# First half of the attention rows mixed through float16 halves, the low halves made by VectorE out of PSUM

## The reference

```python
x = x + 0.5 * ffn(layernorm(x))       # router: 16 experts, top 4
x = x + attention(layernorm(x))
x = x + 0.5 * ffn(layernorm(x))

def attention(x):                     # 8 batches, S = 1024, d = 128
    Q, K, V = x @ Qw, x @ Kw, x @ Vw
    scores = einsum('bqd,bkd->bqk', Q, K) / sqrt(d) + causal mask
    return einsum('bqk,bkd->bqd', softmax(scores), V)
```

## Time and profile before

| | |
|---|---|
| time, median of 3 runs | 674.87 us (673.19 to 675.13) |
| the profiled execution | 673.13 us |
| its span | 671.3 us, so 1.8 us lie around the span |
| PE busy | 634.8 us, 95% |
| DVE busy | 552.5 us, 82% |
| ACT busy | 554.3 us, 83% |
| POOL busy | 521.8 us, 78% |

### The profile page before, as it was taken

One profiled execution on the slowest core, in us unless ns is written; L12 is line 12 of the kernel. 1 busy time (PEld: TensorE's weight loads), 2 busy tenths in 40 slices (PEclk: granted clock), 3 DMA queues, 4 the chain that ended last, 5 costly groups with the idle time before them and its releaser, 6 DMA issues.

```text
span 671.3 us, 15215 instructions
## 1 busy us (share of the span) xinstructions
PE 634.8 (95%) x3395; PEld 493.3 (73%) x3395; DVE 552.5 (82%) x2562; ACT 554.3 (83%) x1187; POOL 521.8 (78%) x411
## 2 busy tenths in 40 slices
PE   4689999999999999699998999999999999999997
PEld 3557777777777776578787787777777777777775
DVE  4898999898998986568777688878999898899863
ACT  3479889898888899888888877679888888988975
POOL 3379989889999887756556656569999989998976
PEclk9999999999999999899999999999999999999999
DMA  9866677765678760344344443975678887677882
GB/s 240 200 149 129 143 153 160 162 145 129 143 151 172 154 139 1 68 94 85 72 94 78 86 90 59 209 146 129 146 171 169 178 172 165 145 168 166 178 173 73
DMA packets 107801, 92.05 MB, mean 137 GB/s; under 512 B 59488, under 2 KB 73456, under 8 KB 107760
## 3 DMA queue, kind: packets, MB, share of 16 engines
q1 hardware_dynamic: 105552, 91.00, 64.1%
q10 hardware_dynamic: 2208, 0.59, 0.4%
HBM read 72.70 MB, written 5.24 MB: 116 GB/s over the span
## 4 chain that ended last, share of the span: by engine, by line
PE 76%; DVE 10%; ACT 5%; issue 4%; POOL 3%; DMA 1%; POOLq 0%; DVEq 0%; ACTq 0%
PE psum L1373 20%; PE psum L1374 19%; PE psum L1375 19%; PE psum L1446 4%; PE psum L1404 2%; PE psum L1458 2%; DVE w_raw L1255 2%; PE psum L1626 2%; POOL shared L544 1%; PE psum L1420 1%; ACT zn L779 1%; PE psum L1585 1%; PE psum L1610 1%; PE psum L1594 1%; PE psum L1611 1%
## 5 line engine op out<-in xcount | busy, mean ns | idle before, releaser
L452 POOL TENSOR_TENSOR shared_r<-shared,shared_r 128x512 fp32r<-128x512 f32 x256 | 326.4, 1296 | 46.0 <-ACT shared L642 43.5
L1109 DVE SCALAR_TENSOR_TENSOR s_sb<-psum,wb 128x512 f32<-128x512 f32 x256 | 175.6, 688 | 44.7 <-PE psum L1375 25.2
L642 ACT ACTIVATE shared<-s_sb 128x512 f32<-128x512 f32 x288 | 177.8, 619 | 22.8 <-DVE s_sb L1109 22.8
L641 ACT ACTIVATE shared_r<-s_sb 128x512 fp32r<-128x512 f32 x256 | 159.8, 624 | 33.9 <-DVE s_sb L1109 31.9
L1373 PE MATMUL psum<-x_hi,w_hi 128*128 128x512 f32 x288 | 125.8, 437 | 1.5 <-issue 0.9
L1373 PE MATMUL psum<-shared_r,w_hi 128*128 128x512 f32 x256 | 114.6, 447 | 0.5 <-POOL shared_r L452 0.5
L1375 PE MATMUL psum<-x_hi,w_lo 128*128 128x512 f32 x288 | 113.8, 395 | 0.0
L1374 PE MATMUL psum<-x_lo,w_hi 128*128 128x512 f32 x288 | 113.5, 394 | 0.0
L1374 PE MATMUL psum<-shared_r,w_hi 128*128 128x512 f32 x256 | 101.4, 396 | 0.0
L1375 PE MATMUL psum<-shared_r,w_lo 128*128 128x512 f32 x256 | 100.7, 393 | 0.0
L544 POOL TENSOR_TENSOR shared<-s_sb,shared 128x1024 f16<-128x1024 f32 (+3 forms) x32 | 56.7, 1771 | 48.3 <-ACT shared L572 48.3
(11 more groups left out here) (169 smaller groups left out, 1372.4 us busy)
## 6 DMA issues: line engine op xcount, KB each, us to landing
wb<-scratch SPq DMA_DIRECT2D x128, 512.0 KB, 8.1
out<-x_sb SPq DMA_DIRECT2D x16, 256.0 KB, 9.8
x_sb<-in_L_attn_x SPq DMA_DIRECT2D x4, 256.0 KB, 6.4
scratch<-wT SPq DMA_DIRECT2D x32, 32.0 KB, 1.9
w_raw<-in_L_ffn_W ACTq DMA_DIRECT2D x1, 512.0 KB, 6.0
w_raw<-in_L_ffn_W SPq DMA_DIRECT2D x1, 512.0 KB, 6.9
wb<-shared SPq DMA_TRANSPOSE x32, 4.0
w_raw<-in_L_ffn_Ws ACTq DMA_DIRECT2D x1, 64.0 KB, 8.9
```

The costliest lines, as they stand in the source:

```text
L452: nc.gpsimd.tensor_tensor(g_lo[:, j % RING, :], g_f[:, j % RING, :], g_hi[:, j % RING, :].bitcast(F32), ALU.subtract).then_inc(F.glo_done, 1)
L641: nc.scalar.activation(g_hi[:, j % RING, :], s_sb[:, j % RING, :], ACT.Square)
L642: nc.scalar.activation(g_f[:, j % RING, :], s_sb[:, j % RING, :], ACT.Square).then_inc(F.sq_done, 1)
L1109: ins = nc.vector.scalar_tensor_tensor(s_, h_, 0.0, wb[:, u, c, :], ALU.max, ALU.mult)
```

## The change

Four things change, all in attention and all for the soon rows.

1. `pT` keeps the same bytes but holds float16 pairs. ACT's `pT_copy` now writes the high half (scaled by 2^15, undone when the mixed rows are copied out).
2. A new DVE operation for each soon tile, `pT_lo`, reads `tp_ps` and the high half and writes the low half. Tile by tile it reads 512, 384, 256 and 128 columns.
3. PE's `prob_transpose` and `mix` wait for DVE's low half (`pTlo_done`) where they waited for ACT's copy (`pT_done`).
4. `mix` makes three float16 matmuls with `zn16` for each key tile instead of one float32 matmul; for `zn16` POOL's `z16_halves` gets one more wait, and `mix` one.

```diff
-        pT = w_raw[:, 0:HQ * HQ * P].rearrange("p (k q) -> p k q", k=HQ)
+        pT = w_raw[:, 0:HQ * HQ * P].bitcast(F16).rearrange("p (k s q) -> p k s q", k=HQ, s=2)
...
                     wait(pool, A.pair_done[PAIRS[1]], b - 1)
+                    if half == 0:
+                        wait(pool, A.mix_done, b - 1)
...
-                    copy(pT[:, 0:t + 1, q0:q0 + P], tp_ps[:, 0:(t + 1) * P].rearrange("p (k q) -> p k q", q=P)).then_inc(A.pT_done, 1)
+                    copy(pT[:, 0:t + 1, 0, q0:q0 + P], tp_ps[:, 0:(t + 1) * P].rearrange("p (k q) -> p k q", q=P), scale=P_SCALE).then_inc(A.pT_done, 1)
...
+                def pT_lo(b, t):
+
+                    q0 = t * P
+                    v.wait_ge(A.pT_done, HQ * b + SOON.index(t) + 1)
+                    nc.vector.scalar_tensor_tensor(pT[:, 0:t + 1, 1, q0:q0 + P], tp_ps[:, 0:(t + 1) * P].rearrange("p (k q) -> p k q", q=P), P_SCALE,
+                                                   pT[:, 0:t + 1, 0, q0:q0 + P], ALU.mult, ALU.subtract).then_inc(A.pTlo_done, 1)
...
                         for s in range(QT):
+                            if b > 0 and s == 0:
+                                pT_lo(b - 1, SOON[2])
                             row_max(b, s)
+                            if b > 0 and s == 2:
+                                pT_lo(b - 1, SOON[3])
+                            if s == 6:
+                                pT_lo(b, SOON[1])
...
                             if b + 1 < B and s in (5, 7):
                                 q_lo_part(b + 1, (7 - s) // 2, prep_ps)
+                            if s == 5:
+                                pT_lo(b, SOON[0])
...
+                    pT_lo(B - 1, SOON[2])
                     start_ffn(16)
                     finish(B - 2, 0)
                     for c in range(AHEAD):
...
                         lead_ffn(c)
+                        if c == 0:
+                            pT_lo(B - 1, SOON[3])
...
                 def prob_transpose(b, t):
                     pe.wait_ge(A.exp_done, QT * b + PLACE[t] + 1)
-                    wait(pe, A.pT_done, HQ * b + SOON.index(t))
+                    wait(pe, A.pTlo_done, HQ * b + SOON.index(t))
...
                 def mix(b):
 
-                    pe.wait_ge(A.pT_done, HQ * (b + 1))
+                    pe.wait_ge(A.pTlo_done, HQ * (b + 1))
+                    pe.wait_ge(A.z16lo_done[0], b + 1)
...
-                        ins = mm(u_home(b, 0)[:, k * P:], zn(b, 0)[:, k, :], pT[:, k, k * P:], start=(k == 0), stop=(k == HQ - 1))
+                        out_, p_hi, p_lo = u_home(b, 0)[:, k * P:], pT[:, k, 0, k * P:], pT[:, k, 1, k * P:]
+                        mm(out_, zn16[b % 2][:, 0, k, :], p_hi, start=(k == 0), stop=False)
+                        mm(out_, zn16[b % 2][:, 0, k, :], p_lo, start=False, stop=False)
+                        ins = mm(out_, zn16[b % 2][:, 1, k, :], p_hi, start=False, stop=(k == HQ - 1))
```

More of the change, by code:

```diff
@@ L41 @@
 Z_SCALE = 2.0 ** 11
-PROB_SHIFT = 15 * math.log(2.0)
+P_SCALE = 2.0 ** 15
+PROB_SHIFT = math.log(P_SCALE)
 RSQRT_GUESS = 0x5f3759df
@@ L110, in __init__ @@
         self.pT_done = sem("a_pT_done")
+        self.pTlo_done = sem("a_pTlo_done")
         self.mix_done = sem("a_mix_done")
@@ L746, in uT_copy @@
                     wait(sc, A.out_done[half], b)
-                    copy(uT[:, half, :], u_home(b, half), scale=1.0 / Z_SCALE).then_inc(A.uT_done[half], 1)
+                    copy(uT[:, half, :], u_home(b, half), scale=1.0 / Z_SCALE / (P_SCALE if half == 0 else 1.0)).then_inc(A.uT_done[half], 1)
                 def exp(b, s):
```

## The result

The changed kernel takes 693.75 us (median of 4 runs, 690.78 to 696.5), the kernel before 674.66 (4 runs on the same chip, 673.19 to 675.13). The ratio is 1.028, 95% interval 1.025 to 1.031: slower by 19 us. The forecast was slower, 686.5, with 678 to 691 as its range. The direction was right; the time lies 7 us above the forecast and 3 above the range.

What follows compares the result with a forecast made beforehand. PE was 76% of the chain, but ACT's copy ended its idle time ahead of tile 2's transposes. 4.5 + 2.6 + 0.4 + 1.4 + 1.5 + 3.2 - 0.8 = 12.8 us on 673.13, plus 0.6 for run spread: 686.5, range 678 to 691.

Steps and rivals of the forecast that it cites:

- The clock falls as well: Rival: longer PE idle stretches drop TensorE's clock, 1 us a fall; two or three falls, 689; chance 0.17.
- `mix` 2.08 to 1.64: PE's mix gets 0.44 us shorter a batch; in batches 0 to 6 that goes into the wait behind it.
- The link: Tile 2's transposes wait for ACT's copy, then pT_lo: 0.64 us later in each of batches 0 to 6, 4.5 us.
- VectorE's queue in batches 2 and 3: Statistics and row_max stand behind the waiting pT_lo of tile 3, delaying batches 3 and 4 by 1.1 and 1.5: 2.6 us.
- the small ones: pT_lo of tile 0 (0.28 us) in DVE's run up to exp(b, 4); batches 5 and 6 pay, 0.4 us.
- the start of batch 7: row_max(7, 0) must stand behind ACT's copy of tile 1 and its pT_lo: 1.4 us beyond batch 6's link.
- slack covers VectorE's queue outside of batches 2 and 3: row_max(b, 6) ends about 1.0 us after the transposes start, exp(b, 6) began 1.32 after them, so no cost.
- 1.5 + 3.65 - 0.8: Batch 7: pT_lo ahead of scw 1.5 us; mix(7) starts 3.65 later behind pT_lo; a DMA wait swallows 0.8.
- Faster: Rival: PE bounds all of attention, so eight times the 0.44 us of mix comes back, 670.2 us; chance 0.05.
- Links alone: Rival: DVE's queues vanish in unseen waits, leaving 8 x 0.64 less 0.44, +4.7 us, 678.4; chance 0.18.
- `pT_lo` dearer: Rival: pT_lo takes longer than its rows where POOL holds it, 8 x 0.76 us more, 692; chance 0.04.
- That nothing changes: Rival: waiting on pTlo_done is in effect no later than on pT_done and nothing moves, 673.7 us; chance 0.03.

Runs made afterwards that it cites:

- e3_fill: Changed kernel plus unread matmuls inside PE's waits: 18 ahead of tile 2's transposes in batches 0 to 6, 60 ahead of mix(7); 690.14 us.
- e9_fill_all: e3_fill plus 60 more unread matmuls ahead of the w_transpose of batch 7; 689.45 us.
- e10_mix1_fill: Changed kernel with one of mix's three matmuls per key tile, filled as e9_fill_all but 36 unread matmuls instead of 18 ahead of tile 2's transposes; 688.86 us.
- e11_queue_fill: e2_queue with unread matmuls in PE's waits: 12 ahead of tile 2's transposes, 60 ahead of batch 7's w_transpose, 45 ahead of the last values(7, 0); 686.4 us.
- e7_order_norm: Changed kernel with VectorE's order as in e1_order and ScalarE's normalise(b + 2, 1) moved behind the copy of tile 3; 678.97 us.
- e8_best: e7_order_norm with tile 3's pT_lo ahead of the statistics again in batches 0 to 6, and the last pT_lo ahead of start_ffn(17)'s router operations; 677.96 us.
- e1_order: Changed kernel with VectorE's pT_lo of tile 3, tile 1 and the last batch's tile 1 moved behind the work they held back; 686.82 us.
- e2_queue: Kernel before (float32 mix) plus, at pT_lo's four places, a VectorE wait for ACT's copy and an unread reduce of as many columns, no link to PE; 690.61 us.
- e5_mix1: Changed kernel with only one of mix's three matmuls for each key tile, the other two products left out; 699.64 us.
- e4_tiny: Changed kernel with pT_lo cut to 8 columns at the same places with the same waits, low halves left out; 684.82 us.
- e6_before_norm: Kernel before with ScalarE's normalise(b + 2, 1) moved from step 4 to behind the copy of tile 3 at step 5; 672.73 us.
- e12_best_fill: e8_best plus unread matmuls: 12 ahead of tile 2's transposes and 18 ahead of batch 7's w_transpose; 676.68 us.

## Why the prediction was right in direction and too small

**The step that failed** is the rival "The clock falls as well", which was kept out of the likeliest sum and sized as "two or three such falls" at 1 us each. There were five in the profiled execution. Their cost is put together from two stretches: up to batch 7 e3_fill, which has no fall there, has 8.49 us of delay where the changed kernel has 13.72, 5.2; from `mix(7)` to the last stage 12.71 against 10.05, 2.7. Together 7.9 us, a third of the 23 us at half rate and 1.6 a fall. No single run shows the 7.9: e9_fill_all reaches the last stage 5.2 earlier than the changed kernel (20.25 - 15.05), its own fall ahead of batch 7 costs it 1.5 and its filling ahead of `w_transpose` 1.2, which makes 7.9 again. The medians of the filled kernels are 3.6 and 4.3 us lower. The mechanism had been read off at one place, but of the idle stretches to come the forecast named only the longest, ahead of `mix(7)`. Waits of 1.9 to 2.5 us, which the forecast itself gave to tile 2's transposes (1.7 in batch 2), were followed by falls at 282, 326 and 394. The fall at 428 could not be read off in this way: the idle stretches ahead of it, 1.21 and 0.63 us, are no longer than those that did no harm elsewhere. The top of the range, 691, is called two falls in the prediction; at its own price of 1 us two falls are 688.5.

**The waits.** What is left is 20.25 - 7.9 = 12.4, and the forecast's sum was 12.8. The kernel before has a fall of its own in batch 0, which the filled kernels don't; its cost is at most half of its 3.3 us at half rate, so the waits are 12.4 to 14. The delays from b1 on all hold this unknown of up to 1.6 us, so how well b1 agrees in the list below is worth less than how much each later batch adds.

- `mix` 2.08 to 1.64: 1.60. Off the path in batches 0 to 6: right (e10_mix1_fill).
- `pT_lo` 0.69 for 512 columns, never longer: right. Idle time ahead of tile 2's transposes in batch 2: 1.86 for 1.7.
- The link (7 x 0.64), VectorE's queue in batches 2 and 3 (2.6), the small ones (0.4) and the start of batch 7 (1.4): 8.9 together by batch 7; the filled kernel has 8.49. Batch by batch the forecast gives 0.64, 1.28, 3.0, 5.2, 5.8, 6.6, 8.9, measured 0.66, 1.38, 2.84, 4.89, 5.60, 6.75, 8.49.
- But the reason given for the 4.5 was half of it. The forecast said that slack covers VectorE's queue outside of batches 2 and 3. e11_queue_fill has no link and loses nearly the same (7.49 by batch 7 against 8.49). This reads as two paths of about equal length to the next batch, PE through tile 2's transposes and VectorE through `row_max` of step 0 behind `pT_lo` of tile 1. The queue alone was run; the link alone with the clock held was not.
- Batch 7 to `mix(7)`: 1.5 + 3.65 - 0.8 = 4.35; measured 18.11 - 13.72 = 4.39. VectorE waited for the copy of tile 1 (2.14 us, at 446.32), and the router operations came behind, as foreseen. But that the sum fits is luck. `w_transpose` comes 4.15 us behind tile 3's transposes instead of 3.40, 0.75 and not 1.5, and all of it is gone at the `pair` matmuls, 7.44 behind them where it was 7.43: the first and the last term together are nothing, not 0.7. The missing 0.7 is one router operation, 0.88 us long where the same one took 0.18 before. The wait has moved it into an operation of POOL, and the two end together (447.54 and 447.49); before, POOL's had ended at 426.85, 1.4 us ahead of it. Before, then after:

```profile
428.29 0.18 DVE L995 TENSOR_SCALAR scores<-scores 128x64 f32<-128x64 f32 x1
...
425.20 1.65 POOL L544 TENSOR_TENSOR shared<-s_sb,shared 128x768 f16<-128x768 f32 x1 [1.81 <-ACT shared L572]
```

```profile
446.66 0.88 DVE L999 TENSOR_SCALAR scores<-scores 128x64 f32<-128x64 f32 x1
...
446.09 1.40 POOL L548 TENSOR_TENSOR shared<-s_sb,shared 128x640 f16<-128x640 f32 x1 [3.44 <-ACT shared L576]
```

- `mix(7)` itself 0.44 shorter: 0.52 where the clock holds (10.57 to 10.05).

**The other rivals.** Faster: its condition, an earlier copy, was made in e7_order_norm and e8_best, and even so it did not decide. Links alone (678.4): refuted by e11_queue_fill, where the queue without a link costs 11.8 us. `pT_lo` dearer: refuted by its 692 ns; what POOL held up was the router operation behind it. That nothing changes: refuted.

## What to carry to other kernels

Where a change lengthens waits on TensorE, put the granted clock into the likeliest sum, and count every place whose idle stretch comes near the one in the trace behind which the clock fell as a possible fall. When a new operation waits on an engine with an ordered list, ask what stands behind it in that list and place it after its data is there; here that was worth 7 us, the falls of the clock that went with it included, and the order of the engine that makes the data another 8. A cheaper operation inside a wait is worth nothing, or less than nothing.

## What the runs showed of the hardware

- Removing two thirds of `mix` made the kernel 5.9 us slower, and 36 matmuls without a reader in each of seven waits, with 120 more in batch 7, made that kernel 10.8 us faster. Both go with the granted clock in attention, 0.90 and 1.00 (277 to 470).
- The length of one idle stretch does not decide alone: in the changed kernel the clock fell behind idle stretches of 2.45, 1.86, 2.30 and 4.20 us, and held behind one of 1.91 at 439.55; in e1_order it held behind one of 2.27 at 391.55. Nor is a fall the same in each execution. The changed kernel's fall at 428 lies behind stretches of 1.21 and 0.63 us ahead of two products of batch 7. e3_fill and e9_fill_all have the same two stretches there (at 420.8 and 423.0); the clock held in the one and fell in the other.
- VectorE's router operation of 0.18 us (`scores` to `scores`, 64 columns) takes 0.88 us in after, e2_queue, e3_fill, e5_mix1, e9_fill_all, e10_mix1_fill and e11_queue_fill and 1.14 in e4_tiny, where it starts inside POOL's 1.40 us on the probabilities, and ends 0.05 us behind that each time. Where the two do not meet it takes 0.18 or 0.19 (before, e1_order, e6_before_norm, e7_order_norm, e8_best, e12_best_fill). `pT_lo`, which reads PSUM, was never longer than 0.69. A wait in an ordered list can push work behind it into such a meeting.
- The Trainium skill (TensorE: Matmul & The Clock Gate, Terms) puts the cost of throttled time at half of it; by that the 23 us are an estimated 11.5. The account above has 7.9 for them. The rest presumably fell into waits that were there anyway, which no run here shows.
